# Sixteen groups of a two-part block on one core: the orders of all engines laid anew over five groups per turn, with own orders for the first and last turns, and the weight preparation in three parts over the first turns

## The chip, the cores and the metric

The kernel runs on one core of a Trainium2 chip. The metric is the device time of one execution in microseconds (us). The kernel before took 771.79 us in the median of three runs (770.97 to 773.9).

## The reference, cut to what matters

The input is 32 sequences of 256 tokens with 128 channels, in float32. Two blocks follow each other, each with a normalization before and after it and a residual.

```python
def _L0_attn_ref(x, ...):                       # RWKV block with spiking neurons
    x = x + lif(time_mix(layer_norm(x, ln1_s, ln1_b), tmk, tmv, tmr, w_decay, u_first, Wk, Wv, Wr, Wo))
    x = x + lif(channel_mix(layer_norm(x, ln2_s, ln2_b), f_tmk, f_tmr, fWk, fWr, fWv))
    return x

def _L0_ffn_ref(x, ...):                        # ternary weights, 512 hidden
    h = silu(_tlin(x, w1_w, w1_s)) * _tlin(x, w2_w, w2_s)
    h = gelu(_tlin(h, h1_w, h1_s), approximate=False)
    h = gelu(_tlin(h, h2_w, h2_s), approximate=False)
    return _tlin(h, w3_w, w3_s)

x = x + _layernorm(_L0_attn_ref(_layernorm(x), ...))
x = x + _layernorm(_L0_ffn_ref(_layernorm(x), ...))
```

`time_mix` mixes each token with the one before it, forms k, v and r by three products, runs `wkv` (a recurrence over time with a running maximum), multiplies by sigmoid(r) and by Wo. `lif` is a neuron whose voltage halves at each step, gains the input, fires at 1 and is then reset. `channel_mix` is r and a squared ReLU of a 128 to 512 product, and a product back.

## The kernel before, in words

**Tiling.** The 32 sequences are 16 groups of two. A group is 512 tokens by 128 channels: one 128x512 float32 tile in token layout (four blocks of 128 tokens) or in channel layout (channels on the partitions, time along the row). Each group goes through a chain of some 130 steps on four engines.

**The steps of one group**, by the names that the profile, the orders and the prediction use:

- stats, moments (`bn1`, `mv1`) on VectorE (DVE), variance and power -1/2 (`var1`, `rstd1`) on GpSimd (POOL), norm (`n1` on DVE, `x1` on POOL), then four transposes into `p_turn` (TensorE, PE), `z1` (ScalarE, ACT), the difference in time `d1` (POOL), and three mixes `mixed1` (DVE).
- k, r and v products (`p_k`, `p_m0`, `p_v`), the scan for the maximum `o` and the excess `e` (DVE), the exponents `factors` (DVE and ACT) and two exps of 128x1024 each (ACT), `bv` (two products with `p_v`), the two sums over time `pq` (two scans each), their products with a factor `nd` (POOL), the denominator and the numerator (DVE), log and exp(-x) of the denominator for the inverse `y` (ACT), and `yr` (DVE).
- the Wo product into `p_k`, `h_in0` (ACT), the voltage scans `volt0`, the spikes and their count `fired0` (DVE), a product with ones that adds the counts (`p_m`), the flag `fired_all0`, a branch of POOL on it (`neurons`, which runs the exact neuron only if anything fired), the spikes transposed (`p_spk`), and the residual `x2`. Norm 2 (`bn2`, `mv2`, `rstd2`, `n2`, `z2`, `d2`, `mixed2`) follows.
- channel mix: an r product (`p_m1`), four k products (`channel_k`, alternating over `p_m0` and `p_m1`), ReLU and square (`kk`), four products back (`channel_v`, all into `p_m0`), the second neuron (`h_in1`, `volt1`, `fired1`), `x3`, norm 3 and the residual with the input on POOL (`n3`, `xres`), norm 4 (`n4`), and `f0_hi` (ACT) and `f0_lo` (DVE): the input of the feed-forward part as a sum of a rounded and a rest part.
- feed-forward: four times a gate and a value product (`gate_products`: `p_f0`, `p_f1` for even, `p_v`, `p_m1` for odd), silu (`gate`), `swiglu` (`hid`), two hidden layers of four outputs (`hidden`), each output eight matmuls of the rest and rounded parts (`a_hi`, `a_lo`, then `b_hi`, `b_lo`) with the weights, gelu, the last product (16 pairs of 128x128) into `p_turn`, `f_out`, norm 5, `y_out` and the store.

**Turns.** A turn holds the steps of several groups in different stages. In the kernel before, turn i works on the early part of group i+1, the wkv part of i, the channel part of i-1, the feed-forward part of i-2 and the end of i-3. Every engine has its order written out by hand in `first_turn`, `turn` and `last_turn`; `schedule` (L315) calls them for turns -1 to 18. Turns 4 to 13 are a hardware loop of two turns per pass; the others are written out. `first_turn` serves turns below 2, `last_turn` those from 16.

**What couples the engines.** Each engine takes its instructions in order and waits on semaphores. PSUM has eight banks, all in use: `p_turn` is shared by the transposes 1, 2, 4 and the last product, `p_m0` by the r product, the two neuron sums, `channel_k` 0 and 2 and all of `channel_v`, `p_v` by v and the odd gates. ACT must load a function table for exp and log (L641), for silu (L644) and for gelu and tanh (L647): three loads in each full turn.

**Weights.** The hidden weights come in three parts. ACT rounds a part (`w_hi`, L617), DVE forms the rest (`w_lo`, L922) and counts what is not zero in it (L929). The count goes through a product with ones to a flag on which PE branches once (L1684 to L1691): with a rest of zero it takes the copy of the program with half as many products. The third part is staged in `hid`, where the second has been.

Of the kernel before, what the change touches and what calls it, by code (L numbers as in the profile page):

```python
# [33 lines left out]
NO_MAXIMUM = -1e38  # L34

# [18 lines left out]

def wait(eng, sem, count):

    if not isinstance(count, int) or count > 0:
        eng.wait_ge(sem, count)


def build(nc, x_in, vec_in, scale_in, mix_in, ffn_in, out):
# [7 lines left out]
    assert C == P and N == 512 and 3 * HB + 2 * HB * HB == MB and GROUPS % 2 == 0  # L69
# [5 lines left out]
    with ExitStack() as ctx:  # L75
# [116 lines left out]
        s_stage = [sem(f"s_stage{k}") for k in range(2)]  # L192
# [4 lines left out]
        s_hi_w = sem("s_hi_w")  # L197
        s_lo_w = sem("s_lo_w")
        s_rest = sem("s_rest")
        s_rest1 = sem("s_rest1")  # L200
        s_quarter = sem("s_quarter")
# [22 lines left out]
        s_bv = sem("s_bv")  # L224
# [79 lines left out]
        parts = [(kk, H1, HB * HB), (hid, H2, HB * HB), (hid, W1, 2 * HB)]  # L304
# [10 lines left out]
        def schedule(fori, first_turn, turn, last_turn, first=-1, last=GROUPS + 2):  # L315

            def on(i):
                return {"shift_k": i + 1 < GROUPS, "wkv": 0 <= i < GROUPS, "channel": 0 <= i - 1 < GROUPS,
                        "ffn": 0 <= i - 2 < GROUPS, "store": 0 <= i - 3 < GROUPS, "weights": i + 1 < len(parts)}
            loop = range(4, GROUPS - 2)  # L320
            for i in range(first, last + 1):
                if i == loop[0]:
                    with fori(loop[0] // 2, len(loop) // 2 + loop[0] // 2) as pair:
                        turn(pair, 0, on(4))
                        turn(pair, 1, on(5))
# [6 lines left out]
        def _(sp):  # L332
# [30 lines left out]
            def turn(pair, step, on):  # L363
                g = Group(pair, step)

                if not isinstance(g.n, int) or 1 <= g.n < GROUPS - 2:
                    load_a(Group(pair, step + 2))
                if on["wkv"] and (not isinstance(g.n, int) or g.n > 0):
                    load_b(g)
                if on["store"]:  # L370
                    f = Group(pair, step - 3)
                    sp.wait_ge(s_y_out, f.n + 1)
                    sp.dma_start(out_tiles[f.n], y_out[:, :, :]).then_inc(s_stored, 16)
# [6 lines left out]
        def _(pool):  # L380
# [24 lines left out]


# [100 lines left out]
            def first_turn(pair, step, on):  # L507

                nxt, g, c = (Group(pair, step + k) for k in (1, 0, -1))
                if on["shift_k"]:  # L510
                    variance(1, nxt)
                    rstd(1, nxt)
                if on["wkv"]:
                    weighted_sum(g, 1)
                    weighted_sum(g, 0)
                if on["channel"]:
                    neurons(1, c)
                if on["shift_k"]:
                    shift_1(nxt)
                if on["wkv"]:  # L520
                    neurons(0, g)
                if on["channel"]:
                    variance(3, c)
                    rstd(3, c)
                    norm_3(c)
                    residual_3(c)
                if on["wkv"]:
                    variance(2, g)
                    rstd(2, g)
                if on["channel"]:  # L530
                    variance(4, c)
                    rstd(4, c)
                if on["wkv"]:
                    shift_2(g)
                if on["shift_k"]:
                    norm_0(nxt)

            def turn(pair, step, on):
                nxt, g, c, f, done = (Group(pair, step + k) for k in (1, 0, -1, -2, -3))
                if on["shift_k"]:  # L540
                    variance(1, nxt)
                    rstd(1, nxt)
                if on["wkv"]:
                    weighted_sum(g, 1)
                    weighted_sum(g, 0)
                if on["store"]:
                    variance(5, done)
                    rstd(5, done)
                    norm_5(done)
                if on["shift_k"]:  # L550
                    shift_1(nxt)
                if on["channel"]:
                    neurons(1, c)
                if on["ffn"]:
                    low(1, f, 1)
                if on["store"]:
                    residual_5(done)
                if on["wkv"]:
                    neurons(0, g)
                if on["channel"]:  # L560
                    variance(3, c)
                if on["ffn"]:
                    low(2, f, 1)
                if on["channel"]:
                    rstd(3, c)
                if on["wkv"]:
                    variance(2, g)
                    rstd(2, g)
                if on["channel"]:
                    norm_3(c)  # L570
                    residual_3(c)
                if on["wkv"]:
                    shift_2(g)
                if on["channel"]:
                    variance(4, c)
                    rstd(4, c)
                if on["shift_k"]:
                    norm_0(nxt)

            def last_turn(pair, step, on):  # L580

                c, f, done = (Group(pair, step + k) for k in (-1, -2, -3))
                if on["store"]:
                    variance(5, done)
                if on["ffn"]:
                    low(1, f, 1)
                if on["store"]:
                    rstd(5, done)
                    norm_5(done)
                if on["channel"]:  # L590
                    neurons(1, c)
                if on["ffn"]:
                    low(2, f, 1)
                if on["store"]:
                    residual_5(done)
                if on["channel"]:
                    variance(3, c)
                    rstd(3, c)
                    norm_3(c)
                    residual_3(c)  # L600
                    variance(4, c)
                    rstd(4, c)
# [5 lines left out]
        def _(act):  # L608
# [4 lines left out]
            def high_weights(i):  # L613

                staged, blocks = part(i + 1)
                act.wait_ge(s_stage[min(i + 1, 1)], 16 * max(i + 1, 1))
                act.activation(w_hi[:, blocks], staged, ACT.Copy).then_inc(s_hi_w, 1)  # L617
# [1109 lines left out]
```

## Time and profile before

| what | value |
|---|---|
| median of three runs | 771.79 us |
| the profiled execution: its own time | 772.1 us |
| its span, first to last instruction | 770.3 us |
| PE busy | 633.8 us (82%) |
| DVE busy | 605.6 us (79%) |
| ACT busy | 478.7 us (62%) |
| POOL busy | 433.5 us (56%) |
| mean granted TensorE clock | 0.949 |

The table shows no engine that is full. The shares are means over a start of some 100 us, a long even middle and an end, so they have to be read by stage. PE's busy time counts modelled ends, and the spans on POOL are rough.

### The profile page before, as it was taken

To read this page: it belongs to the slowest core of one execution; us is meant where nothing else is said; L and a number is where in the kernel's file an instruction comes from. 1 tells how busy PE (TensorE), PEld (TensorE's weight loads), DVE (VectorE), ACT (ScalarE), POOL (GpSimd) and SP (SyncE) were. 2 spreads that over 40 slices of the span, in tenths; PEclk is the share of its full clock that TensorE was granted. 3 is DMA by queue.
4 is the path that set the end of the run, shared out by engine and by line. 5 is a ranking of instruction groups with operands and counts; after the bars stand their busy time and mean duration, and the time that the engine had idled before them with its cause. 6 is when DMAs were issued, how large, how long until landed. Compare 5 with 4: busy or idle time off the path is not lost. (4 is left out here: it accounts for less than half of the span.)

```text
span 770.3 us, 10620 instructions
## 1 busy us (share of the span) xinstructions
PE 633.8 (82%) x2563; PEld 398.7 (52%) x2563; DVE 605.6 (79%) x1558; ACT 478.7 (62%) x711; POOL 433.5 (56%) x560
## 2 busy tenths in 40 slices
PE   3175399889898989889898989899898979888894
PEld 1022146565564646455564646565565646465663
DVE  5888777988879697897979797988979797955340
ACT  2543376767666674767667675857677676847461
POOL 4333526666574765666674767566665757553432
PEclk9567689999999999999999999999999999999998
DMA  6020000000000000000000000000000000000000
GB/s 205 4 69 0 29 1 2 27 16 28 14 29 15 12 16 14 27 14 27 14 27 14 27 9 5 27 14 27 14 27 14 14 15 14 15 1 1 14 15 14
DMA packets 26528, 16.70 MB, mean 22 GB/s; under 512 B 1152, under 2 KB 25728, under 8 KB 26240
## 3 DMA queue, kind: packets, MB, share of 16 engines
q1 hardware_dynamic: 26496, 16.34, 7.0%
q8 instruction: 12, 0.20, 0.1%
q14 instruction: 20, 0.16, 0.1%
HBM read 12.14 MB, written 4.19 MB: 21 GB/s over the span
## 5 line engine op out<-in xcount | busy, mean ns | idle before, releaser
L718 ACT ACTIVATE hid<-p_f,scale 128x512 f32<-128x512 f32 x128 | 87.9, 687 | 119.5 <-PE p_f L1490 119.5
L412 POOL TENSOR_TENSOR var<-mv,eps_row 128x4 f32<-128x4 f32 x64 | 34.4, 537 | 188.4 <-DVE mv L945 188.4
L1490 PE MATMUL p_f<-a_lo,w_hi 128*128 128x512 f32 x256 | 112.1, 438 | 9.3 <-DVE a_lo L295 8.6
L1490 PE MATMUL p_f<-b_lo,w_hi 128*128 128x512 f32 x256 | 109.1, 426 | 2.8 <-DVE b_lo L295 1.2
L1490 PE MATMUL p_f<-a_hi,w_hi 128*128 128x512 f32 x256 | 104.6, 409 | 0.0
L1490 PE MATMUL p_f<-b_hi,w_hi 128*128 128x512 f32 x256 | 101.1, 395 | 0.0
L425 POOL TENSOR_TENSOR rstd<-var,minus_half 128x4 f32<-128x4 f32 x64 | 81.9, 1279 | 2.5
L1475 PE MATMUL p_m<-kk,mix 128*128 128x512 f32 x128 | 64.9, 613 | 9.4 <-ACT kk L692 9.2
L1466 PE MATMUL p_m<-mixed,mix 128*128 128x512 f32 x128 | 65.1, 633 | 6.5 <-issue 6.1
L1490 PEld LDWEIGHTS p_f<-a_lo,w_hi 128*128 128x128 f32 x256 | 50.5, 197 | 30.7 <-DVE a_lo L295 13.5
L1537 PEld LDWEIGHTS p_turn<-w,hid 128*128 128x128 f32 x512 | 58.7, 192 | 10.7 <-issue 9.3
L1537 PE MATMUL p_turn<-w,hid 128*128 128x128 f32 x512 | 60.3, 276 | 2.2 <-issue 1.5
L441 POOL TENSOR_TENSOR nd<-factors,pq 128x512 f32<-128x512 f32 x32 | 42.5, 1329 | 31.7 <-DVE pq L1025 31.7
L1490 PEld LDWEIGHTS p_f<-b_lo,w_hi 128*128 128x128 f32 x256 | 48.1, 188 | 23.3 <-issue 10.7
L1368 PE MATMUL p_turn<-ident,n 128*128 128x128 f32 x192 | 32.2, 292 | 32.5 <-DVE n L961 32.5
L1490 PEld LDWEIGHTS p_f<-a_hi,w_hi 128*128 128x128 f32 x256 | 50.6, 198 | 9.0 <-issue 0.2
L1368 PEld LDWEIGHTS p_turn<-ident,n 128*128 128x128 f32 x192 | 22.3, 145 | 63.4 <-DVE n L961 54.8
L1490 PEld LDWEIGHTS p_f<-b_hi,w_hi 128*128 128x128 f32 x256 | 48.2, 188 | 12.5 <-issue 3.1
L688 ACT ACTIVATE kk<-p_m 128x512 f32<-128x512 f32 x64 | 37.8, 590 | 25.2 <-PE p_m L1466 25.1
L712 ACT ACTIVATE a_hi<-hid 128x512 fp32r<-128x512 f32 x64 | 40.5, 632 | 20.5 <-DVE hid L1145 20.0
L295 DVE TENSOR_TENSOR a_lo<-hid,a_hi 128x512 fp32r<-128x512 f32 x48 | 45.6, 971 | 0.7
L1054 DVE TENSOR_TENSOR_SCAN volt<-half_row,h_in 128x256 f32<-128x256 f32 x64 | 41.9, 695 | 2.2 <-ACT h_in L670 1.7
(132 smaller groups left out, 1541.9 us busy)
## 6 DMA issues: line engine op xcount, KB each, us to landing
xa<-in_x SPq DMA_DIRECT2D x16, 256.0 KB, 2.9
xb<-in_x SPq DMA_DIRECT2D x16, 256.0 KB, 3.2
out<-y_out SPq DMA_DIRECT2D x16, 256.0 KB, 2.3
kk<-in_ffn SPq DMA_DIRECT2D x1, 1024.0 KB, 6.6
hid<-in_ffn SPq DMA_DIRECT2D x1, 1024.0 KB, 9.0
mix<-in_mix SPq DMA_DIRECT2D x1, 512.0 KB, 6.6
hid<-in_ffn SPq DMA_DIRECT2D x1, 512.0 KB, 3.8
mix<-in_mix SPq DMA_DIRECT2D x1, 320.0 KB, 4.2
```

The lines of the kernel that those rows point to most:

```text
L295: eng.tensor_tensor(lo[:, m], hid[:, m], hi[:, m].bitcast(F32), ALU.subtract).then_inc(done, 1)
L425: pool.tensor_tensor(rstds[n][:, :], var[n][:, :], minus_half[:, 0], ALU.pow).then_inc(s_rstd[n], 1)
L441: pool.tensor_tensor(nd[:, n], factors[:, 0], pq[:, n, :, 0:T], ALU.mult).then_inc(s_apq, 1)
L688: act.activation(kk[:, m], p_m[m % 2][:, :], ACT.Relu).then_inc(s_relu, 1)
L712: act.activation(dst[:, m], hid[:, m], ACT.Copy).then_inc(s_hi[layer], 1)
L718: act.activation(hid[:, m], p_f[m % 2][:, :], ACT.Gelu, scale=scale[:, 1 + layer, m:m + 1]).then_inc(s_gelu[layer], 1)
L1054: last = dve.tensor_tensor_scan(volt[k][:, b], half_row[:, :], h_in[k][:, b], 0.0, ALU.mult, ALU.add)
L1368: last = pe.transpose(p_turn[:, j * P:(j + 1) * P], tiles[:, j], ident[:, :])
L1466: pe.matmul(p_m[m % 2][:, :], mix[:, MIX["fWk"] + m], flat(mixed2[:, 1]), start=True, stop=True).then_inc(s_fk, 1)
L1475: last = pe.matmul(p_m[0][:, :], mix[:, MIX["fWv"] + m], kk[:, m], start=(m == 0), stop=(m == HB - 1))
L1490: last = pe.matmul(out_, w[:, b], x[:, k], start=(k == 0 and t == 0), stop=(k == n - 1 and t == len(terms) - 1))
L1537: last = pe.matmul(p_turn[:, j * P:(j + 1) * P], hid[:, m, j * P:(j + 1) * P], w3[:, m], start=(m == 0), stop=(m == HB - 1))
```

## The change

All five engines get new orders. A turn now takes steps of group i+1 (stats 1 only), i (norm 1, transposes 1), i-1 (k, r, v, wkv up to the ratio), i-2 (from `yr` and the Wo product to `channel_k` 3 and `channel_v` 2), i-3 (from `channel_k`'s last ReLU to the gate products 2) and i-4 (from gate 3 to `f_out` and the store). The turns run from -2 to 19; the loop holds turns 6 to 13; `first_turn` serves turns below 3, and PE's branch on the weights' rest stands ahead of turn 3 instead of turn 2.

```diff
-        def schedule(fori, first_turn, turn, last_turn, first=-1, last=GROUPS + 2):
+        def schedule(fori, first_turn, turn, last_turn, first=-2, last=GROUPS + 3):
 
             def on(i):
-                return {"shift_k": i + 1 < GROUPS, "wkv": 0 <= i < GROUPS, "channel": 0 <= i - 1 < GROUPS,
-                        "ffn": 0 <= i - 2 < GROUPS, "store": 0 <= i - 3 < GROUPS, "weights": i + 1 < len(parts)}
-            loop = range(4, GROUPS - 2)
+                return {k: 0 <= i - k < GROUPS for k in range(-2, 5)}
+
+            def groups(pair, step):
+                return {k: Group(pair, step - k) for k in range(-2, 5)}
+            loop = range(6, GROUPS - 2)
...
-                    which = first_turn if i < 2 else turn if i < GROUPS else last_turn
-                    which(i // 2, i % 2, on(i))
+                    which = first_turn if i < 3 else turn if i < GROUPS else last_turn
+                    which(groups(i // 2, i % 2), on(i))
```

The weight preparation: the third part is staged in `gate` and its load waits for nothing; the count on DVE becomes a sum of absolute values on ACT; each part has its own semaphores.

```diff
-        parts = [(kk, H1, HB * HB), (hid, H2, HB * HB), (hid, W1, 2 * HB)]
+        parts = [(kk, H1, HB * HB), (hid, H2, HB * HB), (gate, W1, 2 * HB)]
...
-                if n == 2:
-                    sp.wait_ge(s_rest, n)
-                sp.dma_start(staged, ffn_in[:, blocks]).then_inc(s_stage[min(n, 1)], 16)
+                sp.dma_start(staged, ffn_in[:, blocks]).then_inc(s_stage[n], 16)
...
+            def rest_weights(k):
+
+                staged, blocks = part(k)
+                act.wait_ge(s_lo_w[k], 1)
+                act.activation(staged, w_lo[:, blocks].bitcast(F32), ACT.Abs,
+                               accum_out=w_rest[:, k:k + 1]).then_inc(s_rest[k], 1)
...
-                dve.tensor_scalar(staged, w_lo[:, blocks].bitcast(F32), 0.0, None, ALU.not_equal, ALU.add,
-                                  accum_out=w_rest[:, i + 1:i + 2]).then_inc(s_rest, 1)
```

Small edits: `gate_products` is cut into `to_gate` and `to_value`, which stand apart in PE's order; `bv` has a semaphore for each half; the second moments of norm 1 wait for `neg_mean1` instead of `x1`, and the variance on POOL waits for `x1`; on PE the waits for a free PSUM bank are formed by a new function `after`, in the written-out turns with up to five waits more on an instruction than in the loop:

```diff
+def after(eng, sem, n, per=1, nth=1):
+
+    if isinstance(n, int):
+        if n < 0:
+            return
+        if n >= GROUPS_IN_ALL:
+            n, nth = GROUPS_IN_ALL - 1, per
+    eng.wait_ge(sem, per * n + nth)
```

Of the new orders a few lines stand for all (PE in `turn`):

```diff
+                def turn(g, on):
+
+                    if on[4]:
+                        to_gate(g[4], 3)
+                        to_value(g[4], 3)
+                    if on[3]:
+                        channel_v(g[3], 3)
+                    if on[2]:
+                        out_product(g[2])
...
```

**DVE, the end of wkv.** The first piece is DVE's order before, in a written-out turn, from the moments of norm 1 to `yr`; `pq<-factors` and `pq<-factors,bv` are the two sums over time, `nd` the denominator and then the numerator and the ratio.

```order
L945 BN_AGGR mv1<-bn1 128x2 x4
L1014 TENSOR_TENSOR bv<-factors,p_v 128x512 x2
L1025 SCALAR_TENSOR_TENSOR pq<-factors 128x256 x2
L1025 SCALAR_TENSOR_TENSOR pq<-factors,bv 128x256 x2
L961 TENSOR_SCALAR n1<-xa,mv1,rstd1 128x128 x4
L1032 TENSOR_TENSOR nd<-nd,factors 128x512
```

The same place now, from `f0_lo` (the last step of norm 4's input) on:

```order
L1173 TENSOR_TENSOR f0_lo<-p_turn,f0_hi 128x512
L1001 TENSOR_SCALAR n1<-xa,mv1,rstd1 128x128 x4
L1065 SCALAR_TENSOR_TENSOR pq<-factors 128x256 x2
L1054 TENSOR_TENSOR bv<-factors,p_v 128x512 x2
L1072 TENSOR_TENSOR nd<-nd,factors 128x512
L1065 SCALAR_TENSOR_TENSOR pq<-factors,bv 128x256 x2
```

The first sum moved ahead of `bv`; the second sum and the norm `n1` no longer stand between the first sum and the denominator.

**ACT, the tables.** Before, from the last gelu to the first ReLU of the next turn (`factors` are the two exps):

```order
L718 ACTIVATE hid<-p_f1,scale 128x512
L630 ACTIVATE tanh_r<-p_m0 128x512
L681 ACTIVATE tanh_r2<-p_m1 128x512
L697 ACTIVATE f0_hi<-p_turn 128x512
L641 ACT_TABLE_LOAD
L655 ACTIVATE factors<-factors 128x1024
L688 ACTIVATE kk<-p_m0 128x512
```

Now:

```order
L735 ACTIVATE hid<-p_f1,scale 128x512
L697 ACTIVATE tanh_r2<-p_m1 128x512
L657 ACT_TABLE_LOAD
L704 ACTIVATE kk<-p_m0 128x512
L713 ACTIVATE f0_hi<-p_turn 128x512
L668 ACTIVATE factors<-factors 128x1024
```

The table for exp is loaded ahead of `f0_hi` instead of behind it.

**ACT, the start of the gelu stretch.** Before, `h_in0` stood between the silus, ahead of the gelu table; now this is the order there:

```order
L729 ACTIVATE a_hi<-hid 128x512 x2
L663 ACT_TABLE_LOAD
L640 ACTIVATE z1<-p_turn,vec 128x2x256
L686 ACTIVATE h_in0<-p_k 128x512
L735 ACTIVATE hid<-p_f0,scale 128x512
```

`z1` and `h_in0` moved behind the last two roundings and the gelu table.

## Rows read from the trace of the kernel before

**Rows 1.** Busy time by stretch: length, busy time per engine, granted clock, DMA.
```profile
50.00:100.00 50.00, 28.43 (x56) 11.19 (x57) 37.23 (x104) 21.70 (x30) 20.71 (x30) 0.67 0.12 37
223.52:267.67 44.15, 39.46 (x161) 25.30 (x160) 36.99 (x96) 29.26 (x45) 27.01 (x34) 0.96 0.06 19
354.50:397.14 42.64, 38.05 (x162) 24.28 (x161) 36.98 (x96) 29.24 (x45) 27.28 (x34) 1.00 0.06 18
```

**Rows 2.** Timeline of ACT, turns 6 and 7: start, us, instruction, idle before.
```profile
366.01 1.28 ACT L644 ACT_TABLE_LOAD   x1
370.42 0.58 ACT L670 ACTIVATE h_in<-p_k 128x512 f32<-128x512 f32 x1
396.52 0.60 ACT L697 ACTIVATE f_hi<-p_turn 128x512 fp32r<-128x512 f32 x1 [0.61 <-PE p_turn L1368]
399.87 1.05 ACT L652 ACTIVATE factors<-factors 128x1024 f32<-128x1024 f32 x1
406.90 0.63 ACT L661 ACTIVATE y<-nd 128x512 f32<-128x512 f32 x1 [1.12 <-DVE nd L1032]
408.59 1.28 ACT L644 ACT_TABLE_LOAD   x1
```

**Rows 3.** Timeline of DVE over the same stretch.
```profile
376.28 1.26 DVE L1054 TENSOR_TENSOR_SCAN volt<-half_row,h_in 128x256 f32<-128x256 f32 x2
378.79 0.13 DVE L1069 COPY fired_all<-p_m 1x1 f32<-1x1 f32 x1
382.62 0.69 DVE L1082 TENSOR_TENSOR x<-p_spk,x 128x512 f32<-128x512 bf16 x1 [0.77 <-PE p_spk L1440]
384.82 0.38 DVE L945 BATCH_NORM_AGGREGATE mv<-bn 128x2 f32<-128x6 f32 x4
400.95 1.27 DVE L1025 TENSOR_TENSOR_SCAN pq<-factors 128x256 f32<-128x256 f32 x2
402.14 2.19 DVE L1025 TENSOR_TENSOR_SCAN pq<-factors,bv 128x256 f32<-128x256 f32 x2
404.25 2.01 DVE L961 TENSOR_SCALAR n<-xa,mv,rstd 128x128 f32<-128x128 f32 x4
```

**Rows 4.** Groups by line: count, then busy us, mean ns of one, idle before.
```profile
L704 ACT ACTIVATE gate<-p_f,scale 128x512 f32<-128x512 f32 x32 | 21.9, 685 | 4.3 <-PE p_f L1490 3.8
L1145 DVE SCALAR_TENSOR_TENSOR hid<-p_f,scale,gate 128x512 f32<-128x512 f32 x32 | 23.4, 731 | 12.7 <-ACT gate L704 12.7
L712 ACT ACTIVATE a_hi<-hid 128x512 fp32r<-128x512 f32 x64 | 40.5, 632 | 20.5 <-DVE hid L1145 20.0
```

**Rows 5.** Timeline of POOL, the first wkv product; and DVE's first norm.
```profile
402.31 1.48 POOL L441 TENSOR_TENSOR nd<-factors,pq 128x512 f32<-128x512 f32 x1 [0.58 <-DVE pq L1025]
...
8.93 1.12 DVE L961 TENSOR_SCALAR n<-xa,mv,rstd 128x128 f32<-128x128 f32 x4 [2.61 <-POOL rstd L421]
```

**Rows 6.** Timeline of PE: channel and last products, a pair of hidden products.
```profile
353.69 1.98 PE L1466 MATMUL p_m<-mixed,mix 128*128 128x512 f32 x4
355.51 3.73 PE L1537 MATMUL p_turn<-w,hid 128*128 128x128 f32 x32
374.59 0.40 PE L1490 MATMUL p_f<-a_lo,w_hi 128*128 128x512 f32 x1
374.82 0.40 PE L1490 MATMUL p_f<-a_hi,w_hi 128*128 128x512 f32 x1
```

**Rows 7.** Timeline of PE, behind its branch; DVE's weight steps of the first part.
```profile
96.21 6.02 PE L1466 MATMUL p_m<-mixed,mix 128*128 128x512 f32 x8 [6.14 <-issue]
...
10.88 2.29 DVE L922 TENSOR_TENSOR w_lo<-kk,w_hi 128x2048 fp32r<-128x2048 f32 x1 [0.84 <-ACT w_hi L617]
16.15 2.27 DVE L929 TENSOR_SCALAR_CACHE_REDUCE kk<-w_lo 128x2048 f32<-128x2048 f32 x1
```

**Rows 8.** Timeline of DVE and ACT: marks of the start and of the end.
```profile
32.54 0.69 DVE L1048 TENSOR_TENSOR yr<-nd,y 128x512 f32<-128x512 f32 x1
98.79 1.05 ACT L652 ACTIVATE factors<-factors 128x1024 f32<-128x1024 f32 x1
655.53 1.05 ACT L652 ACTIVATE factors<-factors 128x1024 f32<-128x1024 f32 x1
734.40 0.69 ACT L704 ACTIVATE gate<-p_f,scale 128x512 f32<-128x512 f32 x1 [3.84 <-PE p_f L1490]
```

More of the change, by code:

```diff
@@ L223, in build @@
         s_expB = sem("s_expB")
-        s_bv = sem("s_bv")
+        s_bv = [sem(f"s_bv{k}") for k in range(2)]
         s_pq = sem("s_pq")
@@ L361, in _ @@
             sp.dma_start(w3[:, :, :], ffn_in[:, W3:W3 + HB]).then_inc(s_w3_in, 16)
[L363 to L373, printed above, removed]
+            def turn(g, on):
+                if not isinstance(g[0].n, int) or 1 <= g[0].n < GROUPS - 2:
+                    load_a(g[-2])
+                if on[0] and (not isinstance(g[0].n, int) or g[0].n > 0):
+                    load_b(g[0])
+                if on[4]:
+                    sp.wait_ge(s_y_out, g[4].n + 1)
+                    sp.dma_start(out_tiles[g[4].n], y_out[:, :, :]).then_inc(s_stored, 16)
             schedule(sp.Fori, turn, turn, turn)
@@ L505, in low @@
                 split_low(pool, layer, g, m)
[L507 to L602, printed above, removed]
+            def first_turn(g, on):
+                if on[2]:
+                    neurons(0, g[2])
+                if on[0]:
+                    variance(1, g[0])
+                    rstd(1, g[0])
+                if on[2]:
+                    variance(2, g[2])
+                    rstd(2, g[2])
+                    shift_2(g[2])
+                if on[1]:
+                    weighted_sum(g[1], 1)
+                if on[0]:
+                    norm_0(g[0])
+                if on[1]:
+                    weighted_sum(g[1], 0)
+                if on[2]:
+                    neurons(1, g[2])
+                if on[0]:
+                    shift_1(g[0])
@@ new lines, in scaled_w3, with low_weights @@
+            def scaled_w3():
+                dve.wait_ge(s_w3_in, 16)
+                dve.wait_ge(s_w3_row, 1)
+                for m in range(HB):
+                    last = dve.tensor_tensor(w3[:, m], w3[:, m], p_f[1][:, 0:P], ALU.mult)
+                last.then_inc(s_w3_scaled, 1)
+            def low_weights(k):
+                staged, blocks = part(k)
+                dve.wait_ge(s_hi_w[k], 1)
+                dve.tensor_tensor(w_lo[:, blocks], staged, w_hi[:, blocks].bitcast(F32),
+                                  ALU.subtract).then_inc(s_lo_w[k], 1)
@@ L935, in statistics, with rest_max @@
+            def rest_max():
+                for k in range(len(parts)):
+                    dve.wait_ge(s_rest[k], 1)
+                dve.tensor_reduce(w_rest1[:, :], w_rest[:, :], AX_X, ALU.max).then_inc(s_rest1, 1)
             def statistics(n, g, bn, tiles):
@@ L1397, in time_product @@
                         pe.wait_ge(s_mix_in, 16)
-                    for s in freed:
-                        wait(pe, s, count)
                     pe.matmul(bank_[:, :], mix[:, MIX[name]], flat(mixed1[:, n]), start=True,
```

1504 lines of the change are left out of this document (911 added, 593 removed).

## The prediction

> **What bounds the kernel now.** I read the page's shares first, then busy time by stretch, then one even turn engine by engine in the timelines. No engine is full. In an even turn of 42.64 us PE is busy 38.05, DVE 36.98, ACT 29.24, POOL 27.28 [rows 1]. So neither one engine nor the DMA sets the turn, but a ring of steps that runs over all four and closes once per turn. I follow it from one silu table on ACT (366.01) to the next (408.59), 42.58 us [rows 2, 3]:
>
> - a: table to `h_in0` 4.41 (370.42).
> - b: to the start of `volt0` 5.86 (376.28). `h_in0` is long ready; DVE stands in front of it with swiglus and rest parts.
> - c: to the end of the flag `fired_all0` 2.64 (378.92).
> - d: to `x2` 3.70 (382.62). The flag goes through POOL's branch, then the spikes wait on PE behind two hidden outputs.
> - e: to the end of `mv2` 2.58 (385.20).
> - f: norm 3, residual, norm 4 up to the end of `f0_hi` 11.92 (397.12).
> - g: exp table, two exps, sums, POOL's product, denominator, log, exp, 11.47 to the next table.
>
> The reader is to see in g that the denominator is late because `bv`, two sums (1.27 and 2.19) and a norm (2.01) stand in a row on DVE, and that ACT waits 1.12 for it before the log [rows 2, 3]. Every wait is small; they are spread, and the ring has no slack.
>
> **The even turn after the change.** I add up the same ring in the new order, with the durations of the rows.
>
> - a becomes 9.2. Table 1.28, silu 0, a ReLU and silu 1 to 3.0, swiglu 1 to 4.0, then four DVE steps of about 0.66 from start to start to 6.6, the last rounding to 7.3, gelu table to 8.6, `z1` to 9.2 (silu 0.69, swiglu 0.73, rounding 0.63 [rows 4]; a start on a full engine comes some 0.1 before the end of the step ahead of it). The worsening of 4.8 is what the move of `h_in0` behind the gelu table costs.
> - b becomes 1.8. The rest parts and the first neuron are done meanwhile; `volt0` starts at 11.0. The loss of a is taken back here: a and b are 11.0 against 10.3.
> - c becomes 3.4: as before 2.6, and one more rest part (0.67) between scan and spikes.
> - d becomes 1.6. The flag comes at 14.4, POOL's branch takes about 0.9, and PE stands in `hidden(1,3)` until 15.4; before, the spikes waited behind `hidden(1,1)` and `hidden(1,2)`. Saves 2.1.
> - e becomes 3.4: a rest part more between stats and moments. Costs 0.8.
> - f stays 11.9.
> - g becomes 6.9. The exp table (1.28) now runs while PE transposes norm 4. Behind `f0_hi` stand only the two exps (2.0), the first sum (1.2), POOL's product (1.48 [rows 5]), the denominator (0.65), log and exp (1.25) and hops of 0.1. The second sum and the norm, 4.1 us of DVE in rows 3, are out of the way. Saves 4.6.
>
> Sum 9.2 + 1.8 + 3.4 + 1.6 + 3.4 + 11.9 + 6.9 = 38.2. Now the other engines must fit in. PE has, from start to start, 13 float32 products of 0.91 (two in 1.82 [rows 6]; 0.86 in a row of mixed ones), 80 products of 0.23, a last product of 3.7, three transposes of 0.5 and 0.6 of small ones: at least 36 us, against 38.05 of "busy", which holds pauses after a wait. In the walk PE stands for 0.9 at the fourth pair of `hidden(2,0)` (its rest part is the third of three that DVE makes between stats 2 and moments 2) and 0.8 at the second r product: 37.7, just below the ring. DVE has 36.98 less what contention it loses: `n1` takes 2.01 beside POOL's products and 1.12 alone [rows 3, 5], the second sum 2.19 against 1.27 for the first; I take 2 us off. I add 0.3 for missed hops: 38.5 per turn. Bounds: 36.9, if PE alone sets the turn (36 and the first of its two pauses), and 42.6, if the saved 4.1 is eaten.
>
> **Start.** Mark: the end of the exps of group 2, 99.84 before [rows 8]. Now the first part's rest (2.29 [rows 7]) stands where its count (2.27) stood, and the counts go to ACT, at its 1.9 for 2048 columns an idle engine there. `yr` of group 0 comes at 33.3 (before 32.5 [rows 8]), exps of group 1 end at 57.9, one after before. Then PE has seven channel products in a row from 53 on, the first at the low level (the mean granted clock there was 0.67 [rows 1]) and so near 1.8 each, the later ones at 0.9: PE reaches the branch at about 64.5; its pause of 6.14 [rows 7] is paid as before, once, and the Wo product of group 1 starts at 72. From Wo product to end of exps the ring has 27 us, but PE is emptier and slower there; with 25 the mark is 97. Bounds 93 (no pause felt by group 1) and 104 (pause and low clock both on the path).
>
> **Middle.** 13 turns from group 2 to group 15: 13 x 38.5 = 500.5. Before: 656.58 - 99.84 = 556.7, 42.8 each, three of them 44.2 instead of 42.6.
>
> **End.** Before, 77.8 from the exps of group 15 to the first silu of group 15 (734.40 [rows 8]) and 35.9 from there to 770.3. Now: 5.1 to the next silu table, a turn without wkv of 35, then 32 until gate 0 of group 15, which still stands behind the last product of group 14; in sum 72. The last 35.9 is the chain of one group and stays. 108 against 113.7; bounds 104 and 114.
>
> **Sum.** 97 + 500.5 + 108 = 705.5 of span. The profiled execution had 772.1 on a span of 770.3, so 1.8 more: 707.3. One turn at the slower 44.2 kind (1.6, three before [rows 1]) gives 709. The profiled 772.1 is 0.3 above the median of 771.79, which I neglect. **Edits taken at nothing.** The third weight part no longer waits for the second's count: its load was hidden and is more so. The variance of norm 1 waits for `x1` of the group before, which POOL itself made a turn earlier. On SP the load of `xb` for group i waits for `xres` of i-2, which POOL now makes only in turn i+1, some 25 us in, and the store of i-4 is queued behind it: it is issued at 25 + 38.5 = 63, and POOL overwrites `y_out` at 14 in turn i+2, so at 91. That cover is 28 us. If it went, POOL's residual would stand, and behind it the next first neuron. No wait is added in the loop; in the written-out turns up to five satisfied waits stand on an instruction of PE. The trace shows up to three of them on one; I bound the rest with nothing and 0.2 for each of 30 places in nine turns, a fifth of them on the path: 0 to 11, and take nothing, as three cost nothing visible.
>
> **The rivals.**
>
> *Contention stays.* If the second sum takes 2.19 by itself and not because POOL's product of 1.48 ran beside it, the numerator and the swiglu behind it come 0.9 later, and DVE is back near 36.98 plus its waits. Price 1.3 per turn: 709 + 17 = 726. For it: the trace of before never shows this sum without POOL beside it. Against it: the norm, the same shape, goes from 1.12 to 2.01 in that company. The Trainium skill, SBUF — State Buffer, "SBUF: two separate sides", says that a DVE instruction with two SBUF inputs and a GpSimd instruction that reads SBUF exclude each other for a whole instruction, and that one with a single SBUF input outside the two-port modes does not. By that rule POOL's product costs `bv` (one input in PSUM) nothing, and this rival falls; the trace agrees for the sum, as far as two durations can.
>
> *The clock.* Three turns before had a granted clock of 0.96 and took 1.6 more [rows 1], with the same idle gaps as their neighbours. If that comes in each of the 13 turns: 709 + 12 x 1.6 = 728. Against it: PE will have fewer and shorter gaps. The Trainium skill, TensorE: Matmul & The Clock Gate, Part 1, says that low is the default and activity releases the full clock; by that rule the denser order has no such turn, and the sum would be 707.
>
> *Half the gain.* The ring slips in two or three places that I cut too short (spikes behind a longer hidden output, POOL late by a norm). 41 per turn gives 709 + 32 = 741. For it: POOL's order puts `low(1)` of the next group before `norm_5`, `shift_1` and the second neuron, so a late rounding moves four steps.
>
> *PE sets the turn.* 36.9 per turn: 709 - 21 = 688.
>
> *Slower than before.* The turns now hang together through PE and ACT: value product 1 of group i-3 waits on PE for a ReLU that ACT does behind its silu table, and so behind the inverse `y`, denominator, POOL and DVE; behind it on PE stand gates, the Wo product and all of `hidden`. If that closes late, four engines stand together. It decides from (771.8 - 709) / 13 = 4.8 us per turn, a turn of 43.3; with 44 the time is 780. Against it: in my walk ACT's ReLU is done 0.3 before PE comes to it.
>
> **How the numbers follow.** Forecast 0.62, contention 0.12, clock 0.05, half the gain 0.07, PE alone 0.05: all faster, 0.91. Within 0.5% (which is about what a measurement here can tell from no change) 0.03, slower 0.06. The forecast's own range is 697 to 725 (turn 37.9 to 39.5, start and end 5 either way). The range of 8 in 10 goes from 688 to 738: it holds forecast, contention, clock and PE alone, 0.84, and leaves out the rest, 0.16.
>
> **What would show it.** Right: even turns of 38 to 39 us from silu table to silu table; `pq<-factors,bv` near 1.3 for two and `n1` near 1.1; the log less than 7 us behind `f0_hi`; `x2` within 2 us of the flag; exps of group 2 ending near 97; the pause of about 6 us on PE once, ahead of `channel_v` 3 of group 0. Wrong: PE idle over 3 us in an even turn, POOL late for the second neuron, a turn above 40, or a clock below 1.00 in the even part.

## The result, and the profile after

| | before | after |
|---|---|---|
| median of the runs, us | 772.75 (770.97 to 773.90, 4 runs) | 707.48 (705.99 to 710.65, 4 runs) |
| span of the profiled execution, us | 770.3 | 708.5 |
| ratio after to before | | 0.9163, 95% interval 0.9125 to 0.9201 |

The kernel is 65 us faster; 709 (688 to 738) was forecast. The profiled execution took 710.65 and is the slowest of the four of after; what its trace shows of that is told below.

The shares of the engines first (the page's part 1: busy us, share of the span, instructions):

```profile
PE 613.5 (87%) x2563; PEld 399.0 (56%) x2563; DVE 566.3 (80%) x1552; ACT 482.4 (68%) x718; POOL 438.4 (62%) x560
```

Then busy time by stretch: length, busy time of PE, PEld, DVE, ACT and POOL, granted clock, DMA. The rows are the start, an even turn and the turn before the last; the first two answer to [rows 1].

```profile
50.00:100.00 50.00, 29.27 (x64) 11.77 (x64) 35.72 (x104) 23.68 (x35) 19.91 (x26) 0.70 0.04 11
370.59:408.87 38.28, 36.94 (x162) 24.39 (x160) 35.00 (x98) 29.12 (x44) 27.27 (x35) 1.00 0.07 21
636.44:671.93 35.49, 31.86 (x133) 23.53 (x132) 15.38 (x46) 17.63 (x26) 13.97 (x20) 0.90 0.03 9
```

An even turn went from 42.64 to 38.28. ACT and POOL work as long as they did, DVE is busy 2.0 less, and PE is idle 1.3 instead of 4.6. The 2.0 are four differences between the same instructions in the two traces: the second sum -0.9, norm 1 -0.9, the rest parts `a_lo` -1.1 (the pair at 374.18 took 2.18 before and 1.28 now) and `volt0` +0.9. The ring of the prediction can be read in the timelines of ACT, DVE and POOL (start, us, instruction, idle before), as in [rows 2, 3, 5]:

```profile
370.59 1.28 ACT L660 ACT_TABLE_LOAD   x1
380.25 0.59 ACT L686 ACTIVATE h_in<-p_k 128x512 f32<-128x512 f32 x1
401.69 0.59 ACT L713 ACTIVATE f_hi<-p_turn 128x512 fp32r<-128x512 f32 x1
406.94 0.60 ACT L741 ACTIVATE f_out<-p_turn 128x512 f32<-128x512 f32 x1 [0.24 <-PE p_turn L1792]
407.56 0.63 ACT L677 ACTIVATE y<-nd 128x512 f32<-128x512 f32 x1
408.87 1.28 ACT L660 ACT_TABLE_LOAD   x1
```

```profile
381.27 2.17 DVE L1094 TENSOR_TENSOR_SCAN volt<-half_row,h_in 128x256 f32<-128x256 f32 x2
385.35 0.14 DVE L1109 COPY fired_all<-p_m 1x1 f32<-1x1 f32 x1
387.24 0.69 DVE L1121 TENSOR_TENSOR x<-p_spk,x 128x512 f32<-128x512 bf16 x1 [0.27 <-PE p_spk L1551]
390.09 0.37 DVE L985 BATCH_NORM_AGGREGATE mv<-bn 128x2 f32<-128x6 f32 x4
402.93 1.11 DVE L1001 TENSOR_SCALAR n<-xa,mv,rstd 128x128 f32<-128x128 f32 x4
404.26 1.27 DVE L1065 TENSOR_TENSOR_SCAN pq<-factors 128x256 f32<-128x256 f32 x2 [0.22 <-issue]
406.84 0.69 DVE L1072 TENSOR_TENSOR nd<-nd,factors 128x512 f32<-128x512 f32 x1
407.44 1.27 DVE L1065 TENSOR_TENSOR_SCAN pq<-factors,bv 128x256 f32<-128x256 f32 x2
```

```profile
377.75 3.56 POOL L441 TENSOR_SCALAR f_out<-f_out,neg_mean,rstd 128x128 f32<-128x128 f32 x4
381.28 1.04 POOL L454 TENSOR_TENSOR d<-z 128x512 f32<-128x512 f32 x1
```

The steps a to g of the ring, as the prediction names them, each from row to row:

| | a | b | c | d | e | f | g | turn |
|---|---|---|---|---|---|---|---|---|
| before | 4.41 | 5.86 | 2.64 | 3.70 | 2.58 | 11.92 | 11.47 | 42.58 |
| forecast | 9.2 | 1.8 | 3.4 | 1.6 | 3.4 | 11.9 | 6.9 | 38.2 |
| after | 9.66 | 1.02 | 4.22 | 1.75 | 3.22 | 11.82 | 6.59 | 38.28 |

The reader is to see that the denominator (`nd<-nd,factors`) ends at 407.53 and the log starts at 407.56: ACT's 1.12 of waiting [rows 2] is gone, because the second sum stands behind the denominator and norm 1 ahead of the sums. The copy of `f_out` ends at 407.54, so there two paths arrive together. And `volt0` takes 2.17, against 1.26 before [rows 3], while POOL's shift `d` runs beside it. That was not foreseen.

### The profile page after: what moved, and what is told of

Read it like the earlier page. It is cut to its first block and busy times, and to the rows that moved or that the text cites. A ratio compares the mean times of both kernels' runs of the same rounds, so it can differ in the third digit from the quotient of the medians.

```text
span 708.5 us, 10945 instructions
## 1 busy us (share of the span) xinstructions
PE 613.5 (87%) x2563; PEld 399.0 (56%) x2563; DVE 566.3 (80%) x1552; ACT 482.4 (68%) x718; POOL 438.4 (62%) x560
## 5 line engine op out<-in xcount | busy, mean ns | idle before, releaser
L1634 PE MATMUL p_f<-b_lo,w_hi 128*128 128x512 f32 x256 | 114.0, 445 | 11.0 <-DVE b_lo L306 10.9
L449 POOL TENSOR_TENSOR nd<-factors,pq 128x512 f32<-128x512 f32 x32 | 38.0, 1187 | 102.1 <-DVE pq L1065 102.1
L1634 PE MATMUL p_f<-a_hi,w_hi 128*128 128x512 f32 x256 | 101.0, 394 | 0.0
L433 POOL TENSOR_TENSOR rstd<-var,minus_half 128x4 f32<-128x4 f32 x64 | 75.0, 1172 | 2.5
L1792 PEld LDWEIGHTS p_turn<-w,hid 128*128 128x128 f32 x512 | 61.5, 200 | 12.3 <-DVE f_lo L1173 11.0
L1792 PE MATMUL p_turn<-w,hid 128*128 128x128 f32 x512 | 63.9, 285 | 2.3 <-DVE f_lo L1173 1.4
L441 POOL TENSOR_SCALAR f_out<-f_out,neg_mean,rstd 128x128 f32<-128x128 f32 x64 | 55.0, 871 | 0.8 <-POOL rstd L433 0.8
L1634 PEld LDWEIGHTS p_f<-a_hi,w_hi 128*128 128x128 f32 x256 | 48.3, 189 | 11.2 <-issue 3.6
L1094 DVE TENSOR_TENSOR_SCAN volt<-half_row,h_in 128x256 f32<-128x256 f32 x64 | 50.4, 827 | 2.8 <-ACT h_in L686 2.8
L441 POOL TENSOR_SCALAR x<-xa,neg_mean,rstd 128x128 f32<-128x128 f32 x64 | 45.0, 712 | 0.3 <-POOL rstd L429 0.2
```

The lines of the kernel that those rows point to most:

```text
L433: pool.tensor_tensor(rstds[n][:, :], var[n][:, :], minus_half[:, 0], ALU.pow).then_inc(s_rstd[n], 1)
L441: last = pool.tensor_scalar(out_[:, j], in_[:, j], neg_mean[n][:, j:j + 1], rstd[:, j:j + 1], ALU.add, ALU.mult)
L449: pool.tensor_tensor(nd[:, n], factors[:, 0], pq[:, n, :, 0:T], ALU.mult).then_inc(s_apq, 1)
L1094: last = dve.tensor_tensor_scan(volt[k][:, b], half_row[:, :], h_in[k][:, b], 0.0, ALU.mult, ALU.add)
L1634: last = pe.matmul(out_, w[:, b], x[:, k], start=(k == 0 and t == 0), stop=(k == n - 1 and t == len(terms) - 1))
L1792: last = pe.matmul(p_turn[:, j * P:(j + 1) * P], hid[:, m, j * P:(j + 1) * P], w3[:, m], start=(m == 0), stop=(m == HB - 1))
```

## Experiments

All but two change the kernel after; "per turn" divides the difference of the medians by the 13 turns between the marks of group 2 and group 15. The kernel after was not run again beside them. The kernel before was, each time, with medians of 771.2 to 772.6, so a difference of one or two us between two medians is not sure. The even turn is read from silu table to silu table in each trace.

**The end of DVE's turn put back (`dve_old`).**

```
-    norm_1(g[0])
-    sum_over_time(g[1], 1)
     terms(g[1], 0)
     terms(g[1], 1)
-    denominator(g[1])
+    sum_over_time(g[1], 1)
     sum_over_time(g[1], 0)
+    norm_1(g[0]); denominator(g[1])
```

> The changed kernel with the end of DVE's turn put back as it was: both products bv, then the sum of the denominator, the sum of the numerator, norm 1, the denominator. My theory (the ring closes through the denominator): the denominator stands 1.26 (one more product is ahead of its sum, and the second product too) + 1.27 (the second sum, 2.2 if POOL's product runs beside it) + 1.1 to 2.0 of norm 1 later, less what DVE had idle there (0.2): 2.4 to 4 us per turn, times 13 turns: 739 to 760, against 707.5. The exps would stand as now, and ACT would be idle for that time ahead of the log. Rival (PE sets the turn, with 36.9 of 38.3 busy, and the ring has become slack): under 1 us per turn, 708 to 720. The second sum would show about 2.2 and norm 1 about 2.0 again, since POOL's product runs beside them.

761.2 (758.8 to 761.8): 4.1 per turn, just above the 2.4 to 4 that I expected from the ring, and far from the rival's, under 1. DVE and ACT in its trace:

```profile
437.55 2.19 DVE L1065 TENSOR_TENSOR_SCAN pq<-factors,bv 128x256 f32<-128x256 f32 x2
439.67 2.01 DVE L1001 TENSOR_SCALAR n<-xa,mv,rstd 128x128 f32<-128x128 f32 x4
441.60 0.68 DVE L1072 TENSOR_TENSOR nd<-nd,factors 128x512 f32<-128x512 f32 x1
```

```profile
401.09 1.28 ACT L660 ACT_TABLE_LOAD   x1
411.80 0.59 ACT L686 ACTIVATE h_in<-p_k 128x512 f32<-128x512 f32 x1
432.66 0.59 ACT L713 ACTIVATE f_hi<-p_turn 128x512 fp32r<-128x512 f32 x1
442.31 0.63 ACT L677 ACTIVATE y<-nd 128x512 f32<-128x512 f32 x1 [3.81 <-DVE nd L1072]
443.61 1.28 ACT L660 ACT_TABLE_LOAD   x1
```

ACT stands idle 3.81 ahead of the log, and the turn is 42.52, as long as before, though all other orders are the new ones. The ring theory holds; PE's full row does not set the turn. The two longer durations beside POOL's products are back as well, 2.19 and 2.01. One part of the 4.1 belongs to the new order on ACT: `bv` waits 1.20 here for the exp that it needs, which ACT now makes as the second of the two; in before ACT made it first, and `bv` waited 0.37.

**Nearly the same edit alone on the kernel before (`before_sums`), and with norm 1 ahead of the second sum (`before_norm`).** In after norm 1 stands ahead of both sums, in neither of these two.

```
-    terms(g, 0); terms(g, 1); sum_over_time(g, 1); sum_over_time(g, 0); norm_1(nxt); denominator(g)
+    sum_over_time(g, 1); terms(g, 0); terms(g, 1); denominator(g); sum_over_time(g, 0); norm_1(nxt)
```

and, in `before_norm`, `norm_1(nxt)` ahead of `sum_over_time(g, 0)`.

> The kernel before with one edit in its turns on DVE: sum of the denominator, both products bv, denominator, sum of the numerator, norm 1 (before: products, both sums, norm 1, denominator). This is the edit whose loss cost the changed kernel 4.1 us per turn. If the gains of the parts add up, it is worth that here too: 771 - 13 x 4.1 = 718. By the ring it gives here only what ACT waited for the denominator, 1.12 per turn, since the last ReLU ahead of the log ends at 405.8 with PE in front of it: 1.1 x 13 = 14, 757.

781.6 (ratio to before 1.0143, interval 1.0104 to 1.0182): slower by 1.4%. Both of my numbers were below 772. PE, DVE and ACT in its trace:

```profile
408.27 0.66 PE L1367 MATMUL p_turn<-ident,n 128*128 128x128 f32 x4 [1.51 <-DVE n L961]
```

```profile
401.86 1.27 DVE L1025 TENSOR_TENSOR_SCAN pq<-factors 128x256 f32<-128x256 f32 x2 [1.80 <-ACT factors L652]
406.21 2.01 DVE L961 TENSOR_SCALAR n<-xa,mv,rstd 128x128 f32<-128x128 f32 x4
```

```profile
406.56 0.64 ACT L661 ACTIVATE y<-nd 128x512 f32<-128x512 f32 x1
411.15 0.69 ACT L704 ACTIVATE gate<-p_f,scale 128x512 f32<-128x512 f32 x1 [1.61 <-PE p_f L1489]
```

The log no longer waits, as meant. But norm 1 ends 2 us later, PE's transposes of it stand ahead of the gates, and the first silu waits 1.61 behind its table. Even turns go from 42.6 to 43.1.

> The kernel before with the same edit on DVE as in the last run of it, except that norm 1 stands ahead of the sum of the numerator. Theory: that edit cost 9 us because norm 1 ended 2 us later and PE, in the order of before, has its transposes ahead of channel values and gate 0 (PE idle 1.51 there instead of 0.45, first silu 1.61 late). With norm 1 alone at 1.1 in the old place it ends at 406.2 as before, the log comes 0.3 earlier: 42.2 to 42.6 per turn, 764 to 773. Rival (it is the later numerator and ratio, two places down, that cost it): they are as late here, so 778 to 782 again.

777.4 (771.7 to 783.4; ratio 1.0074, interval 1.0040 to 1.0108): about half the loss is gone, so neither number. The silu starts right behind its table (406.28), norm 1 takes 1.11, but PE and DVE then show:

```profile
410.46 0.47 PE L1490 MATMUL p_f<-f_lo,w_hi 128*128 128x512 f32 x1 [1.54 <-DVE hid L1145]
```

```profile
405.43 0.69 DVE L1037 TENSOR_TENSOR nd<-nd,bv 128x512 f32<-128x512 f32 x1 [0.61 <-POOL nd L441]
409.59 0.72 DVE L1145 SCALAR_TENSOR_TENSOR hid<-p_f,scale,gate 128x512 f32<-128x512 f32 x1
```

The numerator waits for POOL, and with it go ratio, neuron input, `volt1` and only then swiglu 0, for which gate 2 on PE waits 1.54. In the new order swiglu 0 stands right behind the numerator. So the rival was the other half, as far as the trace tells it. Both traces show one thing more, which I had not weighed: DVE stands idle 1.80 ahead of the first sum, which needs both exps, for the second of them. In before, `bv` ran there:

```profile
399.52 1.28 DVE L1014 TENSOR_TENSOR bv<-factors,p_v 128x512 f32<-128x512 f32 x2 [0.37 <-ACT factors L655]
```

In after it is norm 1 that fills this place, and the sum waits 0.22. The two edits on before leave the place empty. So an edit that is worth 4.1 us per turn in the new orders costs some 0.4 to 0.7 in the old ones in two forms close to it; how the form with norm 1 ahead of both sums would do there was not run.

**The exp table behind f0 (`table_late`).**

```
-    exp_table(); relu(g[2], 0); f0(g[3])
+    relu(g[2], 0); f0(g[3]); exp_table()
```

> The changed kernel with the load of the exp table on ACT put behind ReLU 0 and the first f0, ahead of the exps, in turns and last turns. Ring theory: f0_hi comes as now or up to 0.3 earlier (it waits on PE's transpose), then the table's 1.28 stands ahead of the exps and the sums: +1.0 to +1.3 per turn, times 13: 720 to 725, against 707.5. Rival (PE sets the turn, the exps have slack): +0 to +0.3 per turn, 707 to 711.

725.3 (723.7 to 727.3): 1.37 per turn; even turns of 39.5. In its trace the exps follow the table, and the denominator follows them:

```profile
411.36 0.60 ACT L713 ACTIVATE f_hi<-p_turn 128x512 fp32r<-128x512 f32 x1
411.97 1.28 ACT L657 ACT_TABLE_LOAD   x1
418.65 0.63 ACT L677 ACTIVATE y<-nd 128x512 f32<-128x512 f32 x1 [0.37 <-DVE nd L1072]
```

About the whole of the table's 1.28 is on the ring.

**The neuron input ahead of the gelu table (`hin_early`).**

```
+    z_1(g[1]); neuron_input_1(g[2])
     gelu_table()
-    z_1(g[1]); neuron_input_1(g[2])
```

> The changed kernel with z_1 and the neuron input h_in0 of ACT ahead of the gelu table, behind the fourth rounding, in turns. My step a and b: h_in0 is ready 1.3 us earlier but volt0 stands in DVE's row behind swiglus and rest parts until 381.3 whatever ACT does, and the first gelu starts when it did (table and two activations in either order): no change, 707 to 709. Rival (h_in0 holds volt0 as the profile's wait of DVE could be read): volt0 up to 0.5 earlier per turn, 701.

708.05 (706.8 to 711.6), even turns of 38.28. `h_in0` starts 1.39 earlier and `volt0` at 381.30 as it did: what a lost, b had gained.

```profile
378.86 0.58 ACT L686 ACTIVATE h_in<-p_k 128x512 f32<-128x512 f32 x1
```

**A quarter of the last product left out (`pe_less`).** (The `stop` of the sum moves with it.)

```
-    for m in range(HB):
+    for m in range(HB - 1):
```

> The changed kernel whose last product leaves out the fourth block of the hidden values (24 instead of 32 small products, 0.9 us of PE less per group; its output is another one). If PE's full row is what sets the turn beside the ring: -0.9 per turn, 695 to 697. By the ring as I read it, the last product stands on the path only through the output copy that ACT makes ahead of the log, and the denominator comes at the same moment (407.53 and 407.54): the gain is under 0.2 per turn plus 0.9 at the end of the kernel, 704 to 707.

705.5 (701.3 to 707.4). Even turns of 38.17 (silu tables at 371.53 and 409.70): 0.9 us less of work on the engine that is busy 96% of the turn saves 0.1.

**POOL's shift behind its second neuron (`d1_late`).**

```
     norm_5(g[4])
-    shift_1(g[0])
     neurons(1, g[2])
+    shift_1(g[0])
```

> The changed kernel with POOL's shift d1 (difference in time of z_1) behind its second neuron, no longer beside DVE's volt0. volt0 should fall from 2.17 to 1.3 (contention), and the flag fired_all1 behind it comes 0.9 earlier. What it is worth: PE's wait for the spikes behind POOL's branch (0.30) goes, and then hidden(1,3) stands in front of x2's spikes as before, so -0.3 per turn, 703 to 705. If the ring took the whole 0.87: 696. If volt0 stays at 2.1, it is not d1 that slows it but the norm of f_out, and the time stays 707.5.

704.1 (702.3 to 705.7, just apart from after's 705.99 to 710.65); even turns of 37.97. DVE and POOL:

```profile
376.45 1.27 DVE L1094 TENSOR_TENSOR_SCAN volt<-half_row,h_in 128x256 f32<-128x256 f32 x2
```

```profile
378.56 1.04 POOL L454 TENSOR_TENSOR d<-z 128x512 f32<-128x512 f32 x1 [2.06 <-DVE fired_all L1109]
```

The scan is back at 1.27, so it was the shift that slowed it; of 0.90 freed, the turn gets 0.31.

**ReLU 3 later on ACT (`relu_late`).**

```
     silu(g[4], 0)
-    relu(g[3], 3)
     silu(g[4], 1)
-    square(g[3], 3)
     high(1, g[4], 0)
+    relu(g[3], 3); square(g[3], 3)
```

> The changed kernel with ReLU 3 and square 3 of the group in its channel mixing behind silu 1 and the first rounding on ACT, in turns; this is the close of PE and ACT that I named as the way to a slower kernel (value product 1 waits for this ReLU). It ends at 374.5 instead of 373.06, and value product 1 starts 1.4 later than now. The ring runs through swiglu 1 and yr on DVE behind it, which is full from there to volt0: +1.2 to +1.4 per turn, 723 to 726. Rival (the 1.3 us that PE is idle per turn are slack there): +0.3 or less, under 712.

718.9 (717.8 to 719.8), even turns of 39.04: +0.76, or 0.88 per turn by the median, between the two. PE:

```profile
381.55 0.50 PE L1633 MATMUL p_m<-f_lo,w_hi 128*128 128x512 f32 x1 [1.12 <-ACT kk L704]
```

PE waits 1.12 here, and its wait of 0.30 ahead of the spikes (shown below) is gone: part of the delay fell into it. The close of PE and ACT does cost, at somewhat over half of the delay.

**Turn 18 (`tail`).** (The waits of both steps change to fit.)

```
 PE:   + if on[4] and not on[2]: last_product(g[4])
         turn_4(g[3])
 ACT:  + if on[4] and not on[2]: output_tokens(g[4])
         f0(g[3])
```

> The changed kernel whose turn 18 alone differs: PE makes the last product of group 14 ahead of the transposes of norm 4 of group 15, and ACT copies f_out of group 14 ahead of f0 of group 15. Now PE is idle 1.00 and 1.41 ahead of that product, and the product takes 6.78. If it starts 0.8 behind the last hidden product at the full clock it takes 3.7 and ends at 665.9; copy, transposes, f0_hi, f0_lo follow one after the other, gate 0 at 669.5 and the first silu at 669.7 instead of 673.2: -3.5, 704. If the product is slow here too (6.5), the silu comes at 672.7: -0.5, 707.

706.35 (704.5 to 709.5), not to be told from after by the medians. PE in the traces of after, of `hin_early` (which has the same turn 18) and of `tail`:

```profile
664.51 6.78 PE L1792 MATMUL p_turn<-w,hid 128*128 128x128 f32 x32 [1.41 <-DVE f_lo L1173]
```

```profile
664.83 3.84 PE L1792 MATMUL p_turn<-w,hid 128*128 128x128 f32 x32 [1.41 <-DVE f_lo L1173]
```

```profile
661.03 3.81 PE L1794 MATMUL p_turn<-w,hid 128*128 128x128 f32 x32 [0.87 <-ACT hid L735]
```

and the stretches of these products in the first two (same columns as above):

```profile
664.50:671.00 6.50, 6.49 (x31) 6.50 (x32) 0.00 (x0) 0.00 (x0) 0.00 (x0) 0.52 0.01 3
```

```profile
664.50:669.00 4.50, 4.17 (x35) 4.09 (x36) 0.28 (x1) 0.30 (x1) 0.00 (x0) 1.00 0.02 4
```

In after's trace PE was granted 0.52, close to the low one of its two levels (1.2 of 2.4 GHz), behind idle times of 1.00 and 1.41; in `hin_early`, behind the same idle times, 1.00. Turn 18, from silu table to silu table, took 35.49 there and 32.56 (636.76 to 669.32) here. Five more profiles have this product behind the same idle times: `table_late` shows 3.84 at 1.00, and `d1_late`, `relu_late`, `no_branch` and `fewer_waits` show 5.46, 5.32, 5.46 and 5.47 at 0.68 to 0.70. `tail` has the full clock and a turn of 31.83: it gains 3.7 on a slow turn 18 and 0.7 on one at full clock, less 0.3 that its first silu then waits for gate 0.

**No branch (`no_branch`).**

```
-    long_weights = pe.value_load(w_rest_all[0:1, 0:1].bitcast(I32))
-    with pe.If(long_weights != 0): program(True, first=3)
-    with pe.Else(): program(False, first=3)
+    program(False, first=3)
```

> The changed kernel whose PE program runs on in its short form behind turn 2, without the value load and the branch over long weights (the outputs for these inputs are the same). The pause of 5.32 ahead of channel value 3 of group 0 goes. If the ring of group 1 stands behind it, as my start had it (93 against 97 for the mark): -4 to -5.3, 702 to 703.5. If the start is held by ACT and DVE anyway: 707.

704.8 (702.7 to 705.9). PE in after and in it:

```profile
70.86 2.04 PE L1619 MATMUL p_m<-kk,mix 128*128 128x512 f32 x2 [5.32 <-issue]
72.70 1.91 PE L1514 MATMUL p_k<-yr,mix 128*128 128x512 f32 x2
```

```profile
69.28 1.10 PE L1514 MATMUL p_k<-yr,mix 128*128 128x512 f32 x2 [1.93 <-DVE yr L1088]
```

704.8 lies between my two numbers. The pause is 5.32, but the Wo product of group 1 comes only 3.4 earlier, since `yr` is ready no sooner than 69.1. The first silu table comes 3.2 earlier (99.74 instead of 102.94). By itself its place says little, since `d1_late`, `best`, `tail` and `pe_less`, which all have the branch, have it at 100.05, 102.04, 101.96 and 103.87; but from the gelu table at 65.8 to it the way is 33.8 here, and 36.9 to 37.4 in after, `pe_less`, `relu_late`, `tail` and `fewer_waits`.

**No extra waits in PE's written-out turns (`fewer_waits`).** In 34 places:

```
-    if isinstance(g.n, int):
+    if False:
         after(pe, ...)
```

> The changed kernel without the extra waits that PE's written-out turns carry, one wait per buffer as in the loop. I took nothing for them, bounded by 0 and 11 us. Theory: satisfied waits cost PE's queue some tens of ns at most and PE's turns 2 to 5 and 14 to 19 are not bound by it: 706 to 708. Rival (0.2 each, a fifth of them on the path): 702 or less, 696 at the bound.

705.6 (704.5 to 708.1). The silu tables on ACT at the start of turn 14 and of turn 18 stand at 485.42 and 636.44 in after, and here at:

```profile
485.46 1.28 ACT L660 ACT_TABLE_LOAD   x1
635.36 1.28 ACT L660 ACT_TABLE_LOAD   x1
```

Nothing at the start, and 1.1 over four turns of the end. Those four turns are 151.02 long in after, 151.28 in `hin_early`, 150.66 in `tail`, 150.70 in `no_branch` and 149.90 here, and 149.41 in `best` against 149.99 in `d1_late`: the gain is 0.6 to 1.4.

**Three together (`best`):** `d1_late`, `tail` and `fewer_waits`.

> Three edits of earlier runs together on the changed kernel: POOL's d1 behind its second neuron, the last product of group 14 ahead of norm 4's transposes in turn 18, and PE's written-out turns without their extra waits. If they add up: 707.5 - 3.4 (d1) - 1.1 to 3.3 (turn 18: by the medians, and by the profile from the mark on) - 1.1 to 1.9 (waits) = 699 to 702. d1 saves 0.3 per turn in the middle and the other two act behind it, in turns 14 to 18, so they should not share a wait. If PE's waits of turns 14 to 18 are the same that d1 takes away, 703.

702.4 (701.4 to 705.9; ratio to before 0.9106, 0.9075 to 0.9137), just above the sum of the parts (701.9, by 3.4 and 1.1 from the medians and 1.1 for the waits from the trace). It is the fastest of the complete kernels here.

## Why the prediction was right, point by point

**What bounds the turn: right, and shown.** A ring, not an engine: `dve_old` (+4.1 per turn with PE's work unchanged), `table_late` (+1.37) and `pe_less` (-0.1 for 0.9 of PE's work) say the same.

**Sum of the turn: right at 38.2 for 38.28, with errors that cancelled.** g was 0.3 too long, b 0.8 and e 0.2; c was 0.8 too short and a 0.5. The term mis-sized most is c: "as before 2.6, and one more rest part (0.67)" kept `volt0` at 1.26, and it took 2.17. I had weighed the contention of POOL and DVE for the sums and the norm alone. There it went as forecast: the second sum takes 1.27 by itself and norm 1 1.11, and the rival *contention stays* fell. The Trainium skill, SBUF — State Buffer, "SBUF: two separate sides", says that a DVE instruction with two SBUF inputs and a GpSimd instruction that reads SBUF shut each other out for a whole instruction. By that rule the scan (two inputs) is held while `d` (1.04) runs; the trace agrees, 2.17 beside it and 1.27 without. The pairs that the new order makes should have been gone through as the old ones were. The price in the turn is small, since of 0.90 only 0.31 was on the path (`d1_late`). `bv` with POOL's product beside it took 1.26 for two (405.45), no more than in before, as the prediction had it. The 2 us taken off for DVE came out at 2.0 by luck: the sum and the norm gave 1.8 of it, the rest parts another 1.1 that I had not counted, and `volt0` took 0.9 back. The rival *the clock* fell too: the granted clock is 1.00 in the even turn, and no turn of 44 came.

**Where the gain comes from: g, with the other orders around it.** g gave 4.88. `dve_old` is longer than after by 3.77 in g and 1.05 in a. The 1.11 of g that is left is near what the table's place is worth (1.2 to 1.4 in `table_late`). The prediction priced each edit in its new surroundings; alone in the old ones, `before_sums` shows a loss for nearly the same edit.

**PE's idle time:** forecast 1.7 over its 36, at the fourth pair of `hidden(2,0)` and the second r product. In the trace those are 0.67 and 0.23 (at 398.13), and 0.30 stands ahead of the spikes:

```profile
384.32 0.38 PE L1551 MATMUL p_spk<-ident,spikes 128*128 128x128 bf16 x4 [0.30 <-POOLq L488]
390.32 0.47 PE L1634 MATMUL p_f<-b_lo,w_hi 128*128 128x512 f32 x1 [0.67 <-DVE b_lo L306]
```

**Start: 97 forecast, 98.1 measured.** The exps of group 2 end one later than that:

```profile
97.06 1.06 ACT L671 ACTIVATE factors<-factors 128x1024 f32<-128x1024 f32 x1
```

The step "its pause is paid as before, once" was too simple: 5.32, of which 3.4 are felt (`no_branch`). `yr` of group 0 came 2.1 later than forecast (35.40), PE at the branch 1.0 later (65.55 for 64.5), and the Wo product of group 1 0.7 later (72.70 for 72), as the pause was 5.3 and not 6.1. From there to the mark it took 25.4, for my 25. In `hin_early`, `pe_less`, `relu_late`, `tail` and `fewer_waits` the mark stands at 97.1 to 99.0, so an error of one is no more than executions differ by.

**Middle: 13 x 38.5 = 500.5 forecast, 498.3 measured** (the exps of group 15 start at 595.39 and end at 596.45; 38.3 each).

**End: 108 forecast, 112.0 measured in this execution.** The exps of group 15 to the next silu table took 4.8 and the turn without wkv 35.2, as forecast (5.1 and 35), and behind the first silu of group 15 it was 35.3 for 35.9. The term that failed is "then 32 until gate 0 of group 15", at which the sum lets that first silu start: it starts 36.8 after the silu table at 636.44.

```profile
671.32 0.60 ACT L741 ACTIVATE f_out<-p_turn 128x512 f32<-128x512 f32 x1 [7.59 <-PE p_turn L1792]
673.23 0.69 ACT L721 ACTIVATE gate<-p_f,scale 128x512 f32<-128x512 f32 x1
```

Of the 4.8 too many, 2.9 are the last product at a granted clock of 0.52 (6.78 instead of 3.84). The other 1.9 stay at the full clock, where it is 33.9 in `hin_early` (636.76 to 670.62): behind the last product ACT copies `f_out` (0.60) and loads the silu table (1.28) before that silu, and the sum had neither. The 1.6 that I had added for a slower turn in the middle was not needed there, and happened to cover a part of this. Against this execution 709 is 1.6 too low, against the median 1.5 too high. The profiled execution is 3.2 above the median of its kernel; the slow product is of that size, but the other three executions left no trace, so that it is the cause isn't shown.

**Edits taken at nothing:** the extra waits cost some 1 us (0.6 to 1.4), near the low end of 0 to 11.

**The slower rival:** its place was right, its margin was not 0.3 but 0.05 or less (ReLU 3 ends at 373.06, value product 1 starts at 373.11), and its price 0.76 for 1.4 of delay. It would have decided only for a delay of some 8 us, had that slope held; this wasn't tried.

## What to carry to other kernels

Follow one ring of waits through all engines and price an edit in the order in which it will stand: here an edit on DVE is worth 4.1 us per turn with the other engines' new orders, and two forms of it cost 0.4 to 0.7 with the old ones, where they left DVE idle for an exp that ACT made second. When an order changes, list which POOL and DVE instructions newly run beside each other, with the durations that each has alone and in company. An engine at 96% of a turn need not be its bound: take a piece of its work away before believing it.

## What was not expected of the hardware

- The same product of 32 matmuls, behind the same idle times of 1.00 to 1.04 and 1.41 on PE, took 3.84 (two profiles), 5.3 to 5.5 (four) or 6.78 (one) in kernels with the same turn 18; the granted clock was 1.00, 0.68 to 0.70 and 0.52. Why one execution falls to the low level and another doesn't stays open.
- POOL's norm of `f_out` takes 3.56 in the even turn (377.75), with DVE's rest parts and `volt1` beside it, and the same four tiles took 1.73 where DVE stood idle (at 679.79 in after):

```profile
679.79 1.73 POOL L441 TENSOR_SCALAR f_out<-f_out,neg_mean,rstd 128x128 f32<-128x128 f32 x4 [0.20 <-POOL rstd L433]
```

- Up to five satisfied waits on an instruction of PE cost next to nothing: 0.6 to 1.4 us in all for four turns of a full PE.
